# The involution's front joins the block of its taps, and the last experts' weight fold moves into it

## The chip, the cores and the metric

The kernel runs on one core of one Trainium2 chip. The metric is device time in microseconds (us) of one execution of the whole program. One execution was also recorded by the hardware profiler; its trace gives the span between the first and the last instruction, the busy time of each engine and what each instruction waited for. The engines are PE (matmuls), DVE (VectorE), ACT (ScalarE), POOL (GpSimd) and SP (which only issues DMAs here).

## The reference

Four layers, each a convolution-like mixer and then a mixture of experts, on 8 images of 64 channels and 32x32 pixels. The mixer of the last layer is an involution, and the experts of the last layer normalise their input and scale and shift it per expert:

```python
def _involution(x, w_reduce, w_span, gamma, beta):
    r = jnp.einsum('bchw,oc->bohw', x, w_reduce)
    mean = jnp.mean(r, axis=(0, 2, 3), keepdims=True)
    var = jnp.var(r, axis=(0, 2, 3), keepdims=True)
    r = (r - mean) * jax.lax.rsqrt(var + BN_EPS)
    r = r * gamma[None, :, None, None] + beta[None, :, None, None]
    r = jax.nn.relu(r)
    kern = jnp.einsum('bchw,kc->bkhw', r, w_span)          # 9 taps
    xp = jnp.pad(x, ((0, 0), (0, 0), (1, 1), (1, 1)))
    patches = jnp.stack([xp[:, :, i:i + H, j:j + W] for i in range(K) for j in range(K)], axis=2)
    return jnp.einsum('bckhw,bkhw->bchw', patches, kern)
...
# experts of the last layer
xe = xn[None, :, :] * ln_g[:, None, :] + ln_b[:, None, :]
h = jax.nn.gelu(jnp.einsum('end,edh->enh', xe, W1) + b1[:, None, :], approximate=False)
```

The mean and the variance run over all images and pixels, so nothing of the ReLU can begin before all of `r` is there.

## The kernel before, in words

The 8 images lie as 4 pairs (`Q` = 4; two images of 64 channels fill 128 partitions) of 1024 pixels, or as 8 tiles (`NT` = 8) of 512 columns. `X` is the running activation, `XN` its normalised copy; both stay in SBUF, as do all weights `W`.

The program is a row of blocks. In a block each engine has its own instruction list; at its end all engines meet at a barrier, and the next block begins. Inside a block the order on an engine is the written order, and engines wait for each other by counting semaphores.

Four blocks matter here.

**The scan of layer 2** (`mamba_scan`, L2056 to L2367). Its steps end with POOL's `gate`, and SP stores the result of the last image (L2099) and waits until it has landed (L2104). Behind its own scan work PE runs `fold_shift`: 16 matmuls with one moving column (L2041), which multiply the first-layer weights of the last experts by their shift `l3_b`. DVE then runs `fold_gain`: it adds that to the bias (L2049) and multiplies the weights by the gain `l3_g`, one instruction for each of the 8 experts (L2051). None of this is needed before the last experts.

**The involution's front** (a block of its own, L2543 to L2587). PE makes `r` for all 8 tiles in the 8 banks of PSUM (L2548). One ACT instruction copies all 4096 columns to `RR` and sums them (L2559); a matmul with `pairs` adds the sums over the partitions (L2553); DVE makes the negative mean (L2573); ACT squares (L2562); a second matmul; ACT takes the root (L2564), DVE inverts it with one Newton step and makes `SCALE` and `SHIFT` (L2575 to L2583, eight small instructions); one ACT instruction makes the ReLU of all 4096 columns, `RN` (L2566). POOL clears the padded image buffer `XP`.

**The block of the taps** is the block of the last experts (`deep_experts`), with the functions of `involution` called at the head of each engine's list. SP loads each pair's image into `XP` (L2597). For each pair `q` there are 18 taps `n`: two halves of 9, each on 512 columns. PE makes the tap's kernel in one of six PSUM banks (`kern`, L2614) and may run up to four taps ahead of DVE. DVE multiplies the shifted image by it (`scaled`, L2671); three taps (`OWN`) it adds itself (L2685), the others POOL adds (L2719). A half closes with DVE adding its own sum to `X` (L2692), then, after POOL's last addition, POOL's sum (L2694).

Between the taps of the last pair the engines prepare the first two tiles of the experts (`ahead(what, p)`): PE turns X (`in`, L1090), DVE centers (L1272, L1273), ACT squares (L1199), DVE inverts the deviation (`invert`, L1280 to L1298, 17 instructions), PE turns back (L1098), ACT copies (L1204), PE makes router logits (L1106), DVE ranks them (`rank`, L1308 to L1320, 14 instructions), ACT bends (L1209), DVE weighs (L1329 to L1333), PE and ACT turn the weights to rows (L1113, L1216).

**The experts**: PE `up` (L1135), ACT Gelu (L1236), PE `down` (L1158), DVE weighs the result (L1358), POOL adds it up (L1068). ACT's first Gelu waits for the last sum of the involution.

Of the kernel before, what the change touches and what calls it, by code (L numbers as in the profile page):

```python
# [99 lines left out]
def build(nc, x_dram, w_dram, seg_dram, out_dram):  # L100
    ctx = ExitStack()
    with ctx:
# [2433 lines left out]
        def involution():  # L2536
# [6 lines left out]
            with nc.Block() as block:  # L2543
                @block.tensor
                def _(pe):
                    mm = nc.tensor.matmul
                    for t in range(NT):
                        last = mm(PS[:, t, :], w("i_wr"), XN[:, t * T:(t + 1) * T], start=True, stop=True)  # L2548
                    last.then_inc(b_reduced.sem, 1)

                    for src, done in ((TOTAL, 1), (SS, 2)):
                        pe.wait_ge(b_total.sem, b_total.at(done))
                        mm(PS[:, 0, 0:1], w("pairs"), src, start=True, stop=True).then_inc(b_moment.sem, 1)  # L2553

                @block.scalar
                def _(act):
                    f = nc.scalar.activation
                    act.wait_ge(b_reduced.sem, b_reduced.at(1))
                    f(RR, PS[:, :, :].rearrange("p a b -> p (a b)"), ACT.Identity, accum_out=TOTAL)\  # L2559
                        .then_inc(b_total.sem, 1)  # L2560
                    act.wait_ge(b_chain.sem, b_chain.at(1))
                    f(RN, RR, ACT.Square, bias=NEGM, accum_out=SS).then_inc(b_total.sem, 1)  # L2562
                    act.wait_ge(b_moment.sem, b_moment.at(2))
                    f(SD, PS[:, 0, 0:1], ACT.Sqrt, bias=w("eps5")).then_inc(b_total.sem, 1)  # L2564
                    act.wait_ge(b_chain.sem, b_chain.at(9))
                    f(RN, RR, ACT.Relu, bias=SHIFT, scale=SCALE).then_inc(b_total.sem, 1)  # L2566

                @block.vector
                def _(dve):
                    v = nc.vector  # L2570
                    step = Chain(dve, b_chain).step
                    dve.wait_ge(b_moment.sem, b_moment.at(1))
                    step(v.tensor_scalar(NEGM, PS[:, 0, 0:1], -1.0, None, ALU.mult))  # L2573
                    dve.wait_ge(b_total.sem, b_total.at(3))
                    step(v.reciprocal(SD, SD))  # L2575

                    step(v.tensor_scalar(VAR, PS[:, 0, 0:1], w("eps5"), None, ALU.add))
                    step(v.tensor_tensor(SCALE, SD, SD, ALU.mult))
                    step(v.scalar_tensor_tensor(SCALE, SCALE, -0.5, VAR, ALU.mult, ALU.mult))
                    step(v.scalar_tensor_tensor(SD, SCALE, 1.5, SD, ALU.add, ALU.mult))  # L2580
                    step(v.tensor_tensor(SCALE, SD, w("i_gamma"), ALU.mult))
                    step(v.tensor_tensor(SHIFT, NEGM, SCALE, ALU.mult))
# [290 lines left out]
```

## Time and profile before

| | us |
|---|---|
| median of three runs | 1882.13 |
| lowest and highest of them | 1871.58, 1884.21 |
| the profiled execution, device time | 1880.6 |
| its span | 1878.8 |
| PE busy in the span | 1660.1 (88%) |
| DVE busy | 932.2 (50%) |
| ACT busy | 880.7 (47%) |
| POOL busy | 519.1 (28%) |

Busy time is an average over stages that differ. The stretches of the change, between 1118 and 1136 us, 1479 and 1510 us, and 1510 and 1617 us of the span, have to be read by themselves. The profiled execution lies 1.5 us under the median of the runs.

### The profile page before, as it was taken

How to read it: one execution, taken by the hardware profiler on the slowest of the kernel's cores; microseconds unless marked ns; L12 is line 12 of the kernel's file. 1: busy time of each engine (PE TensorE's matmuls, PEld its weight loads, DVE VectorE, ACT ScalarE, POOL GpSimd, SP SyncE). 2: the span in 40 equal slices, each digit the busy share in tenths (PEclk: the TensorE clock that was granted, in tenths of full speed). 3: DMA queues.
4: the chain of work that ended last, by engine and by line, in shares of the span. 5: the costliest groups of instructions: out<-in, count | busy, mean ns of one | idle time of the engine just before them, and what ended most of it. 6: DMA issues, size and time to landing. Idle time of an engine off the chain costs nothing. (4 is left out here: it accounts for less than half of the span.)

```text
span 1878.8 us, 50402 instructions
## 1 busy us (share of the span) xinstructions
PE 1660.1 (88%) x20792; PEld 759.1 (40%) x20792; DVE 932.2 (50%) x2080; ACT 880.7 (47%) x1185; POOL 519.1 (28%) x692
## 2 busy tenths in 40 slices
PE   7988999988998899789788887799999577799998
PEld 3553333333333332233677772333333233333332
DVE  3455544334665556430566654644442278645442
ACT  3225555554555355444445436355555500355554
POOL 0001222220000255501466651122323055122223
PEclk8899999998998799899899987899999799899999
DMA  5004232310000575258234312233232031242422
GB/s 246 12 12 90 48 78 59 71 21 34 12 1 23 124 159 124 50 198 294 63 111 140 125 42 90 46 65 73 54 84 46 0 34 11 50 93 52 94 60 63
DMA packets 88049, 143.24 MB, mean 76 GB/s; under 512 B 35256, under 2 KB 53816, under 8 KB 87824
## 3 DMA queue, kind: packets, MB, share of 16 engines
q1 hardware_dynamic: 87952, 142.02, 29.4%
q8 instruction: 52, 0.85, 0.2%
q14 instruction: 45, 0.37, 0.1%
HBM read 106.07 MB, written 25.44 MB: 70 GB/s over the span
## 5 line engine op out<-in xcount | busy, mean ns | idle before, releaser
L1236 ACT ACTIVATE ARENA<-PS,W 128x1024 f32<-128x1024 f32 x384 | 408.6, 1110 | 340.5 <-PE PS L1158 237.8
L1068 POOL TENSOR_TENSOR ARENA<-ARENA 128x512 f32<-128x512 f32 x168 | 213.0, 1268 | 729.8 <-DVE ARENA L1358 729.8
L1158 PE MATMUL PS<-ARENA,W 128*64 128x512 f32 x1536 | 350.8, 598 | 21.9 <-DVE ARENA L1358 21.9
L1135 PE MATMUL PS<-ARENA,W 64*128 64x512 f32 x1536 | 361.3, 609 | 1.9 <-DVE ARENA L1273 1.9
L1358 DVE SCALAR_TENSOR_TENSOR ARENA<-PS,W,ARENA 128x512 f32<-128x512 f32 x192 | 144.1, 750 | 328.4 <-PE PS L1158 314.0
L1158 PEld LDWEIGHTS PS<-ARENA,W 128*64 128x64 f32 x1536 | 101.9, 136 | 261.1 <-issue 218.6
L1135 PEld LDWEIGHTS PS<-ARENA,W 64*128 64x128 f32 x1536 | 141.1, 188 | 163.8 <-issue 109.0
L581 POOL TENSOR_TENSOR ARENA<-ARENA 128x512 f32<-128x512 f32 x56 | 71.0, 1268 | 292.7 <-DVE ARENA L913 291.1
L2338 PE MATMUL PS<-ARENA 32*32 32x32 f32 x8448 | 104.8, 196 | 6.7 <-issue 6.3
L751 ACT ACTIVATE ARENA<-PS,W 128x1024 f32<-128x1024 f32 x64 | 68.0, 1110 | 70.9 <-PE PS L655 70.9
L2338 PEld LDWEIGHTS PS<-ARENA 32*32 32x32 f32 x8448 | 93.7, 105 | 10.7 <-issue 7.3
L2614 PE MATMUL PS<-ARENA,W 128*128 (+1 forms) x144 | 75.1, 669 | 24.8 <-DVE ARENA L2671 17.3
L2208 ACT ACTIVATE ARENA<-PS 128x512 f32<-128x512 f32 x64 | 38.2, 597 | 94.3 <-PE PS L2312 94.3
L2719 POOL TENSOR_TENSOR ARENA<-ARENA 128x512 f32<-128x512 f32 x40 | 54.9, 1373 | 79.6 <-DVE ARENA L2671 78.1
L677 PE MATMUL PS<-ARENA,W 128*64 128x512 f32 x256 | 65.8, 625 | 8.4 <-DVE ARENA L913 8.4
L913 DVE SCALAR_TENSOR_TENSOR ARENA<-PS,W,ARENA 128x512 f32<-128x512 f32 x64 | 47.1, 749 | 50.8 <-PE PS L677 40.0
L1697 PE MATMUL PS<-ARENA 64*128 64x512 f32 x256 | 71.4, 656 | 0.6 <-ACT ARENA L1750 0.6
L655 PE MATMUL PS<-ARENA,W 64*128 64x512 f32 x256 | 70.3, 671 | 0.0
L1967 PE MATMUL PS<-XN,ARENA 64*128 64x512 f32 (+2 forms) x288 | 63.1, 592 | 4.1 <-DVE ARENA L2014 2.5
L368 PE MATMUL PS<-X,W 128*128 128x512 f32 x80 | 46.7, 694 | 20.0 <-PEq L306 7.2
L1750 ACT ACTIVATE ARENA<-PS 128x1024 f32<-128x1024 f32 x32 | 32.8, 1024 | 67.4 <-PE PS L1697 67.3
L1708 PE MATMUL PS<-ARENA 128*64 128x512 f32 x256 | 62.6, 605 | 0.4 <-ACT ARENA L1754 0.3
(244 smaller groups left out, 2256.3 us busy)
## 6 DMA issues: line engine op xcount, KB each, us to landing
ARENA<-scratch_g SPq DMA_DIRECT2D x64, 768.0 KB, 11.8
ARENA<-scratch_g SPq DMA_DIRECT2D x64, 256.0 KB, 5.9
W<-w_dram SPq DMA_DIRECT2D x1, 7307.5 KB, 24.6
ARENA<-XN SPq DMA_DIRECT2D x12, 512.0 KB, 3.7
ARENA<-XN SPq DMA_DIRECT2D x16, 256.0 KB, 11.2
scratch_x<-ARENA SPq DMA_DIRECT2D x8, 512.0 KB, 3.7
scratch_b<-ARENA SPq DMA_DIRECT2D x8, 512.0 KB, 4.0
scratch_z<-ARENA SPq DMA_DIRECT2D x8, 512.0 KB, 3.9
```

The source lines that it names most:

```text
L581: nc.gpsimd.tensor_tensor(SUM[:, k, :], SUM[:, k, :], TMP[:, e % 2, :], ALU.add)\
L655: last = mm(PS[:, (b % 2) * R + r, :], w(layer + "_w1", b * 128, (b + 1) * 128, half(r)), XE[half(r), k, :], start=True, stop=True)
L677: last = mm(PS[half(r), 4 + e % 2, :], w(layer + "_w2", b * C, (b + 1) * C), H[:, b % 4, r * T:(r + 1) * T], start=part == 0, stop=part == ...
L751: f(H[:, b % 4, :], PS[:, (b % 2) * R:(b % 2) * R + R, :].rearrange("p a b -> p (a b)"), ACT.Gelu, bias=w(layer + "_b1", b, b + 1)).then_i ...
L1068: nc.gpsimd.tensor_tensor(SUM[:, k, :], SUM[:, k, :], TMP[:, e % 2, :], ALU.add)\
L1135: last = mm(PS[:, (u % UPS) * R + r, :], w(layer + "_w1", b * 128, (b + 1) * 128, half(r)), XS[half(r), t % 2, :], start=True, stop=True)
L1158: last = mm(PS[half(r), out_of(e), :], w(layer + "_w2", b * C, (b + 1) * C), H[:, u % HS, r * T:(r + 1) * T], start=part == 0, stop=part = ...
L1236: f(H[:, u % HS, :], PS[:, at:at + R, :].rearrange("p a b -> p (a b)"), ACT.Gelu, bias=w(layer + "_b1", b, b + 1)).then_inc(e_gelu.sem, 1)
L1358: v.scalar_tensor_tensor(by_group(TMP[:, e % 2, :] if e else SUM[:, k, :]), by_group(PS[:, out_of(e), :]), w(layer + "_b2", e, e + 1), WB[ ...
L1697: last = mm(PS[:, 2 * r + h, :], XH[half(r), k, m * TOK:(m + 1) * TOK], XH[half(r), k, h * T:(h + 1) * T], start=True, stop=True)
L2338: last = mm(PS[g, MIXED + k, P + j * CHUNK:P + (j + 1) * CHUNK], XD[g, k, j, u * CHUNK:(u + 1) * CHUNK], M[g, k, u * P + j * CHUNK:u * P + ...
L2614: nc.tensor.matmul(PS[:, n % 6, :], w("i_ws", tap * P, (tap + 1) * P), RN[:, bass.ds(q * S + h * T, T)], start=True, stop=True)\
```

## The change

Three things are done. `fold_shift` and `fold_gain` leave the scan; they now run in the block of the taps, the matmuls in two parts. The front's block is gone: its work stands at the head of the engines' lists in the block of the taps. There the copy and sum are made tile by tile, the root by DVE from a bit pattern and three Newton steps, the ReLU pair by pair, and SP's loads of `XP` wait only for POOL's clearing. The preparation of the first tile is spread over the last two pairs.

```diff
-        def fold_shift(pe):
-            for b in range(E * HIDDEN["L3"]):
+        def fold_shift(part):
+            n = E * HIDDEN["L3"] // 2
+            for b in range(part * n, (part + 1) * n):
...
-            dve.wait_ge(f_shift.sem, f_shift.at(1))
+            dve.wait_ge(f_shift.sem, f_shift.at(2))
...
-                    fold_gain(dve)
...
-                    fold_shift(pe)
...
+                sp.wait_ge(b_cleared.sem, b_cleared.at(1))
+                sp.wait_ge(ln_scaled.sem, ln_scaled.at(0))
                 for k in range(2):
                     load(k, k)
...
+                for t in range(NT):
+                    mm(PS[:, t, :], w("i_wr"), XN[:, t * T:(t + 1) * T], start=True, stop=True)\
+                        .then_inc(b_reduced.sem, 1)
+                pe.wait_ge(b_total.sem, b_total.at(NT))
+                mm(PS[:, 6, 0:NT], w("pairs"), TOTAL, start=True, stop=True).then_inc(b_moment.sem, 1)
+                fold_shift(0)
+                pe.wait_ge(b_total.sem, b_total.at(NT + 1))
+                mm(PS[:, 7, 0:1], w("pairs"), SS, start=True, stop=True).then_inc(b_moment.sem, 1)
+                fold_shift(1)
+                pe.wait_ge(b_total.sem, b_total.at(NT + 2))
+                pe.wait_ge(f_done.sem, f_done.at(1))
+                with pe.Fori(0, Q - 2) as q:
+                    pe.wait_ge(b_total.sem, b_total.at(q + NT + 2))
+                    for n in range(BOTH):
+                        kern(q, n)
...
             def scalar(act, ahead):
+                f = nc.scalar.activation
+                for t in range(NT):
+                    act.wait_ge(b_reduced.sem, b_reduced.at(t + 1))
+                    f(RR[:, t * T:(t + 1) * T], PS[:, t, :], ACT.Identity, accum_out=TOTAL[:, t:t + 1])\
+                        .then_inc(b_total.sem, 1)
+                act.wait_ge(b_chain.sem, b_chain.at(1))
+                f(RN, RR, ACT.Square, bias=NEGM, accum_out=SS).then_inc(b_total.sem, 1)
+                act.wait_ge(b_chain.sem, b_chain.at(MOMENTS))
+                for q in range(Q):
+                    f(RN[:, q * S:(q + 1) * S], RR[:, q * S:(q + 1) * S], ACT.Relu, bias=SHIFT, scale=SCALE)\
+                        .then_inc(b_total.sem, 1)
...
+                dve.wait_ge(b_moment.sem, b_moment.at(1))
+                step(v.tensor_reduce(NEGM, PS[:, 6, 0:NT], AX.X, ALU.add, negate=True))
+                dve.wait_ge(b_moment.sem, b_moment.at(2))
+                step(v.tensor_scalar(VAR, PS[:, 7, 0:1], w("eps5"), None, ALU.add))
+                step(v.tensor_scalar(SD.bitcast(I32), VAR.bitcast(I32), 1, None, ALU.arith_shift_right))
+                step(v.tensor_scalar(SD.bitcast(I32), SD.bitcast(I32), -1, RSQRT_MAGIC, ALU.mult, ALU.add))
+                for n in range(3):
+                    step(v.tensor_tensor(NEWT, SD, SD, ALU.mult))
+                    step(v.scalar_tensor_tensor(NEWT, NEWT, -0.5, VAR, ALU.mult, ALU.mult))
+                    step(v.scalar_tensor_tensor(SD, NEWT, 1.5, SD, ALU.add, ALU.mult))
...
+                fold_gain(dve)
...
-                                ((1, "center", 0), (4, "invert", 0), (10, "rank", 0), (11, "center", 1),
-                                 (13, "weigh", 0), (15, "invert", 1)) if k else ())
+                                ((3, "weigh", 0), (5, "center", 1), (8, "invert", 1)) if k else
+                                ((2, "center", 0), (7, "invert", 0), (17, "rank", 0)))
...
+                pool.wait_ge(e_fold.sem, e_fold.at(0))
+                nc.gpsimd.memset(XP, 0.0).then_inc(b_cleared.sem, 1)
```

On DVE, at the end of the scan's block, the list before reads as follows (L2284 and L2288 are the scan's last steps, L2455 is the first of the next block):

```order
L2284 TENSOR_TENSOR ARENA<-PS,ARENA 128x128 [waits c_mixed]
L2288 SCALAR_TENSOR_TENSOR ARENA<-ARENA,W,PS 128x128 [waits c_summed]
L2049 TENSOR_TENSOR W<-W,PS 128x16 [waits f_shift]
L2051 TENSOR_SCALAR W<-W 128x256 x8
L2085 UNCONDITIONAL_BRANCH
L2451 UNCONDITIONAL_BRANCH [waits barrier_Pool_Activation_PE_DVE_SP_release]
L2455 TENSOR_SCALAR ARENA<-W 128x64
```

And the same place on DVE after the change (line numbers behind it are smaller by three):

```order
L2284 TENSOR_TENSOR ARENA<-PS,ARENA 128x128 [waits c_mixed]
L2288 SCALAR_TENSOR_TENSOR ARENA<-ARENA,W,PS 128x128 [waits c_summed]
L2085 UNCONDITIONAL_BRANCH
L2448 UNCONDITIONAL_BRANCH [waits barrier_Pool_Activation_PE_DVE_SP_release]
L2452 TENSOR_SCALAR ARENA<-W 128x64
```

The nine instructions of the fold stand between the front's chain and the first tap now.

On ACT, the front before, from the copy of `r` to the table of Gelu:

```order
L2559 ACTIVATE ARENA<-PS 128x4096 [waits b_reduced]
L2562 ACTIVATE ARENA<-ARENA 128x4096 [waits b_chain]
L2564 ACT_TABLE_LOAD
L2564 ACTIVATE ARENA<-PS,W 128x1 [waits b_moment]
L2566 ACTIVATE ARENA<-ARENA 128x4096 [waits b_chain]
L2543 UNCONDITIONAL_BRANCH
L1190 UNCONDITIONAL_BRANCH [waits barrier_Pool_Activation_PE_DVE_SP_release]
L2643 ACT_TABLE_LOAD
```

And after the change:

```order
L1190 UNCONDITIONAL_BRANCH [waits barrier_Pool_Activation_PE_DVE_SP_release]
L2625 ACTIVATE ARENA<-PS 128x512 [waits b_reduced] x8
L2628 ACTIVATE ARENA<-ARENA 128x4096 [waits b_chain]
L2631 ACTIVATE ARENA<-ARENA 128x1024 [waits b_chain]
L2631 ACTIVATE ARENA<-ARENA 128x1024 x3
L2633 ACT_TABLE_LOAD
```

The barrier and one table load between the two halves of the front are gone, and the long copy and the long ReLU are cut.

On PE, the last pair before (L2614 are taps, L1098 turns a tile back, L1106 makes logits, L1090 turns a tile in, L1113 turns the weights, L1135 is the first `up`):

```order
L2614 MATMUL PS<-ARENA,W 128x512 [waits i_scaled] x2
L1106 MATMUL PS<-W,ARENA 128x16 [waits ln_normed]
L1106 MATMUL PS<-W,ARENA 128x16 x3
L1090 MATMUL PS<-W,X 128x128 x4
L2614 MATMUL PS<-ARENA,W 128x512 [waits i_scaled] x6
L1113 MATMUL PS<-W,ARENA 64x128 [waits g_split]
L2614 MATMUL PS<-ARENA,W 128x512 [waits i_scaled] x2
L1098 MATMUL PS<-W,ARENA 128x128 [waits ln_scaled]
L1098 MATMUL PS<-W,ARENA 128x128 x3
L1106 MATMUL PS<-W,ARENA 128x16 [waits ln_normed,g_rows]
L1106 MATMUL PS<-W,ARENA 128x16 x3
L1135 MATMUL PS<-ARENA,W 128x512 [waits ln_normed,i_scaled]
```

And after the change, from near the end of the third pair (L2567 are taps; the first twelve below are the third pair's last two and the fourth pair's first ten):

```order
L1090 MATMUL PS<-W,X 128x128 x4
L2567 MATMUL PS<-ARENA,W 128x512 [waits i_scaled] x12
L1113 MATMUL PS<-W,ARENA 64x128 [waits g_split]
L2567 MATMUL PS<-ARENA,W 128x512 [waits i_scaled] x4
L1098 MATMUL PS<-W,ARENA 128x128 [waits ln_scaled]
L1098 MATMUL PS<-W,ARENA 128x128 x3
L2567 MATMUL PS<-ARENA,W 128x512 [waits i_scaled] x2
L1106 MATMUL PS<-W,ARENA 128x16 [waits ln_normed,g_rows]
L1106 MATMUL PS<-W,ARENA 128x16 x3
L2567 MATMUL PS<-ARENA,W 128x512 [waits i_scaled] x2
L1135 MATMUL PS<-ARENA,W 128x512 [waits ln_normed,i_scaled,f_done]
```

Before, all of the second tile's logits stood between the last tap and the first `up`; now two taps stand behind them. On DVE the fourteen instructions of `rank` stand behind the last tap of the third pair, and the seventeen of the second `invert` behind the ninth tap of the fourth, both ahead of the half's closing additions.

## Rows read from the trace of the kernel before

**Rows 1.** Timeline, end of the scan: start, us, engine, line, work, idle before.
```profile
1121.45 6.98 PE L2041 MATMUL PS<-W 64*128 64x1 f32 x32
...
1123.20 0.32 SPq L2099 DMA_DIRECT2D scratch_t<-ARENA  x1
...
1128.56 2.19 DVE L2051 TENSOR_SCALAR W<-W 128x256 f32<-128x256 f32 x8
...
1131.04 13.09 SPq L2389 DMA_DIRECT2D ARENA<-scratch_t  x8
```

**Rows 2.** Waits of SP's queue, 1100 to 1140: waiter, releaser, us, times, longest.
```profile
SPq L2085 <- PEq L2085: 4.9, 1, 4.9
```

**Rows 3.** Timeline, the front up to the first taps.
```profile
1479.04 10.00 PE L2548 MATMUL PS<-XN,W 128*128 128x512 f32 x16 [2.43 <-PEq L358]
...
1489.08 3.58 ACT L2559 ACTIVATE ARENA<-PS 128x4096 f32<-128x4096 f32 x1 [11.09 <-PE PS L2548]
...
1492.81 0.59 PE L2553 MATMUL PS<-ARENA,W 128*128 128x1 f32 x2 [3.76 <-ACT ARENA L2559]
...
1493.63 3.71 ACT L2562 ACTIVATE ARENA<-ARENA 128x4096 f32<-128x4096 f32 x1 [0.87 <-DVE ARENA L2573]
...
1499.10 0.17 DVE L2575 RECIPROCAL ARENA<-ARENA 128x1 f32<-128x1 f32 x1 [5.51 <-ACT ARENA L2564]
...
1500.72 3.80 ACT L2566 ACTIVATE ARENA<-ARENA 128x4096 f32<-128x4096 f32 x1 [1.72 <-DVE ARENA L2583]
...
1505.18 5.46 PE L2614 MATMUL PS<-ARENA,W 128*128 x8 [7.12 <-PEq L2543]
...
1510.28 3.08 DVE L2671 TENSOR_TENSOR ARENA<-ARENA,PS 128x512 f32<-128x512 f32 x5 [9.59 <-DMA ARENA<-XN]
```

**Rows 4.** Windows: stretch, length, busy of PE, PEld, DVE, ACT, POOL, PEclk, DMA, GB/s.
```profile
1121.40:1128.50 7.10, 7.03 (x41) 6.90 (x32) 0.58 (x3) 0.00 (x0) 0.91 (x2) 0.50 0.18 74
...
1479.00:1485.00 6.00, 5.96 (x7) 2.52 (x8) 0.00 (x0) 0.00 (x0) 2.02 (x1) 0.51 0.00 0
...
1489.00:1505.10 16.10, 1.22 (x5) 1.00 (x4) 1.50 (x9) 13.13 (x8) 0.00 (x0) 0.58 0.00 0
1505.10:1508.70 3.60, 3.52 (x4) 1.50 (x5) 0.00 (x0) 0.97 (x1) 0.00 (x0) 0.50 1.10 127
...
1521.70:1526.10 4.40, 4.34 (x6) 1.89 (x7) 4.33 (x7) 0.00 (x0) 2.54 (x2) 0.61 0.00 0
```

**Rows 5.** Timeline, starts of halves of the taps on DVE, and closing additions.
```profile
1532.75 3.07 DVE L2671 TENSOR_TENSOR ARENA<-ARENA,PS 128x512 f32<-128x512 f32 x5
...
1543.49 3.07 DVE L2671 TENSOR_TENSOR ARENA<-ARENA,PS 128x512 f32<-128x512 f32 x5
...
1551.36 1.04 DVE L2692 SCALAR_TENSOR_TENSOR X<-ARENA,X 128x512 f32<-128x512 f32 x1
...
1576.69 1.28 DVE L2671 TENSOR_TENSOR ARENA<-ARENA,PS 128x512 f32<-128x512 f32 x2
...
1593.13 1.28 DVE L2671 TENSOR_TENSOR ARENA<-ARENA,PS 128x512 f32<-128x512 f32 x2
...
1615.63 0.69 DVE L2694 SCALAR_TENSOR_TENSOR X<-ARENA,X 128x512 f32<-128x512 f32 x1 [1.23 <-POOL ARENA L2719]
```

**Rows 6.** Waits, 1500 to 1625.
```profile
DVE X L2694 <- POOL ARENA L2719: 9.8, 8, 1.2
```

**Rows 7.** Timeline: one instruction of `rank` twice, and POOL beside the first.
```profile
1594.49 1.26 POOL L2719 TENSOR_TENSOR ARENA<-ARENA 128x512 f32<-128x512 f32 x1 [2.07 <-DVE ARENA L2671]
1594.58 1.25 DVE L1309 TENSOR_TENSOR ARENA<-ARENA,W 128x64 f32<-128x64 f32 x1
...
1616.49 0.22 DVE L1309 TENSOR_TENSOR ARENA<-ARENA,W 128x64 f32<-128x64 f32 x1
```

**Rows 8.** Timeline, the first `up` matmuls and the first Gelu.
```profile
1615.08 8.78 PE L1135 MATMUL PS<-ARENA,W 64*128 64x512 f32 x32
...
1617.27 1.11 ACT L1236 ACTIVATE ARENA<-PS,W 128x1024 f32<-128x1024 f32 x1 [4.13 <-PE PS L1135]
```

More of the change, by code:

```diff
@@ L2540, in involution @@
             TMP, SUM, OSUM, OTMP = a.take(5, T), a.take(2, T), a.take(T), a.take(T)
-            TOTAL, NEGM, SS, SD, SCALE, SHIFT, VAR = (a.take(1) for _ in range(7))
+            TOTAL = a.take(NT)
+            NEGM, SS, SD, SCALE, SHIFT, VAR, NEWT = (a.take(1) for _ in range(7))
             ROWS_T = T // IMG
[L2543 to L2582, printed above, removed]
-                    step(v.tensor_tensor(SHIFT, SHIFT, w("i_beta"), ALU.add))
-                @block.gpsimd
-                def _(pool):
-                    nc.gpsimd.memset(XP, 0.0).then_inc(b_cleared.sem, 1)
@@ L2616, in kern @@
                         .then_inc(i_kern.sem, 1)
-                with pe.Fori(0, Q - 1) as q:
+                mm = nc.tensor.matmul
+                pe.wait_ge(ln_scaled.sem, ln_scaled.at(0))
+                for t in range(NT):
[3 more added lines that the diff above has]
+                mm(PS[:, 6, 0:NT], w("pairs"), TOTAL, start=True, stop=True).then_inc(b_moment.sem, 1)
@@ L2621, in tensor @@
+                last = Q - 2
                 ahead("in", 0)
-                for n in range(0, 8):
-                    kern(Q - 1, n)
+                for n in range(0, 13):
+                    kern(last, n)
                 ahead("back", 0)
-                kern(Q - 1, 8)
-                kern(Q - 1, 9)
+                kern(last, 13)
+                kern(last, 14)
                 ahead("logits", 0)
+                kern(last, 15)
                 ahead("in", 1)
-                for n in range(10, 16):
-                    kern(Q - 1, n)
+                kern(last, 16)
@@ L2631, in tensor @@
+                kern(last, 17)
+                last = Q - 1
+                for n in range(0, 10):
+                    kern(last, n)
                 ahead("turn", 0)
-                for n in range(16, BOTH):
-                    kern(Q - 1, n)
+                for n in range(10, 14):
+                    kern(last, n)
                 ahead("back", 1)
+                kern(last, 14)
+                kern(last, 15)
                 pe.wait_ge(g_rows.sem, g_rows.at(1))
                 ahead("logits", 1)
+                kern(last, 16)
@@ L2638, in tensor @@
+                kern(last, 17)
+                pe.wait_ge(f_done.sem, f_done.at(1 + E))
                 pe.wait_ge(i_scaled.sem, i_scaled.at(Q * BOTH))
@@ L2656, in vector @@
                 v = nc.vector
+                step = Chain(dve, b_chain).step
+                dve.wait_ge(b_moment.sem, b_moment.at(1))
[8 more added lines that the diff above has]
+                    step(v.scalar_tensor_tensor(SD, NEWT, 1.5, SD, ALU.add, ALU.mult))
+                step(v.tensor_tensor(SCALE, SD, w("i_gamma"), ALU.mult))
+                step(v.tensor_tensor(SHIFT, NEGM, SCALE, ALU.mult))
+                step(v.tensor_tensor(SHIFT, SHIFT, w("i_beta"), ALU.add))
+                fold_gain(dve)
                 def scaled(q, k, n, others):
```

2 lines of the change are left out of this document (added).

## The prediction

> **What bounds the kernel now.** PE is the busiest engine by far, but not in the stretches that change, so I read these by time: first the timeline of the scan's end, then SP's waits there, then the timeline and the clock windows of the involution's front, then the starts of the taps' halves on DVE with the waits that close them, and last the start of the experts. The reader is to see which engine comes last in each.
>
> At the scan's end it is the fold. PE's 16 fold matmuls take 6.98 us, from 1121.45 on, DVE multiplies weights until 1128.56 + 2.19 = 1130.75, and the next block's first DMA starts at 1131.04 [rows 1]. SP has been at the barrier for 4.9 us by then [rows 2], since 1126.1.
>
> In the front nothing runs beside anything: PE, then ACT, PE, DVE, ACT and so on from 1479.04 to 1510.28 [rows 3]. ACT's three passes over 4096 columns are 3.58, 3.71 and 3.80 us of it, and at the end DVE waits not for PE but for the loads of the padded image (idle 9.59, put down to the DMA).
>
> In the taps DVE leads. A half (9 taps) takes 1543.49 - 1532.75 = 10.74 us [rows 5], of which DVE waits 9.8 / 8 = 1.22 for POOL's last addition [rows 6]. The last pair's halves, which hold the preparation of the first two tiles, take 1593.13 - 1576.69 = 16.44 and, to the end of L2694 at 1616.3, 23.2 us [rows 5].
>
> **The change part by part.** The sum is made against the profiled execution, 1880.6 us.
>
> *The fold leaves the scan.* PE then ends at 1121.5, and SP comes last, at 1126.1. The release followed DVE's end by 1131.04 - 1130.75 = 0.29 us, so the next block starts at 1126.4: 4.6 us earlier. Bounds: 4.3 if the barrier takes twice as long behind SP, 4.9 if it takes nothing.
>
> *Front, copy by tiles.* PE needs 10.00 us for the 8 tiles as before. A float32 matmul is two passes in the rows. Seven took 5.96 us at the granted 0.51 [rows 4], 0.85 a pass and 1.7 a tile, the other nine the rest, 0.45 a pass and 0.9 a tile. ACT now follows tile by tile; an eighth of its 3.58 us is 0.45, with a fixed part some 0.6 to 0.8, less than a tile of PE, so only the last tile's stays behind PE: the first moment starts at 1489.8 instead of 1492.81. Gain 3.0.
>
> *Front, the root by DVE.* Before, from the square's start to the ReLU's it took 1500.72 - 1493.63 = 7.1 us. After: the square 3.71 and its read-out 0.2, a matmul of 0.59, and 15 small DVE instructions; eight of them took 1500.72 - 1499.10 = 1.62, 0.2 each, so 3.0. That is 7.5: a loss of 0.4. The ReLU starts at 1489.8 + 0.6 + 0.3 + 7.5 = 1498.2 instead of 1500.72.
>
> *Front, the ReLU by pairs, no barrier.* Only the first quarter is on the path: 3.80 / 4 = 0.95 and some 0.3 fixed, so the first tap's matmul can start at 1499.4 instead of 1505.18.
>
> *The fold in its new place.* Half of the matmuls are 6.98 / 2 = 3.5 us. The first half (1490.4 to 1493.9) lies beside the square, which ends at 1494.5; the second (1495.1 to 1498.6) beside DVE's 15 steps and the first ReLU, until 1499.4. The first tap waits for the bias addition too, and all of PE's taps are queued behind it; it comes at 1498.7, ahead of that ReLU. Then come DVE's 2.19 us of weight products, 1498.9 to 1501.1, while PE makes the first tap. Cost nothing; were that cover gone, 2.2.
>
> *The loads.* They took from the block's start, 1504.8, to 1510.28, 5.5 us. Now they are issued when POOL has cleared `XP`, early in the 20 us of the front; behind them SP has only the loads of the later pairs, which wait for DVE's products. POOL's clearing took 2.02 us, beside PE's first tiles [rows 4]; POOL has nothing else to do there. The 9.59 us are gone, and what is late next is PE.
>
> *PE's clock at the first taps.* Before, PE had four taps ready when the images came. It had made them at the granted 0.50 (1.2 GHz) for 3.6 us first [rows 4]: 1.7 us a tap instead of 0.9. Now DVE waits for each. If the low clock lasts 4.3 us (3.6 and 6.0 are the two rises in [rows 4]), taps 1 to 5 are there after 1.7, 3.4, 4.8, 5.7 and 6.6 us, and DVE ends the fifth at 1499.4 + 7.2 = 1506.6; before, five took 3.08 [rows 3], so that is as if DVE had started at 1503.5. Against 1510.28: **gain 6.8** for the whole front. Bounds: 6.0 with 6 us at the low clock, 9.1 with none (DVE is then held by the weight products).
>
> Here a rule bears. The row: while PE ran these very fold matmuls, busy for 7.03 of 7.10 us, the clock stayed at 0.50 [rows 4]. The Trainium skill says of the gate (TensorE: Matmul & The Clock Gate, "What's actually happening") that "activity releases the throttle"; by it the fold, now just ahead of the taps, would have raised the clock, and the front would gain 9.1. I take the row, and keep the rule as a rival.
>
> *The preparation over two pairs.* DVE's work is the same. In the last two halves it came to 16.44 - 10.74 = 5.7 and 23.2 - 10.74 = 12.5, 18.2 us; with eight plain halves, 85.9, and 2.0 for two halves that PE's clock lengthened (it had fallen, as at 1521.7, [rows 4]) that is the 106.0 from 1510.28 to 1616.3. Now the rank and the second invert stand between a half's last product and its closing additions, so POOL's last addition runs beside them: 1.22 of waiting goes twice, and L2692 runs without POOL beside it, 0.69 like L2694 instead of 1.04 [rows 5], twice. That is 3.1; PE's logits among the taps of the third pair may cost 0.3, and I leave the 2.0 for fallen clocks, since the rank and the inverts leave PE without taps for some us: **gain 2.8**. Bounds: 4.8 if no clock falls. Below nothing, since the moved pieces stand where POOL has additions queued: one instruction of rank took 1.25 beside POOL and 0.22 without [rows 7]; if three pieces lose that once more each, and 0.3 each to PE, it is 2.8 - 4.0 = -1.2.
>
> The row has a rule behind it: by the Trainium skill (SBUF — State Buffer, "Who interferes with whom") a DVE instruction with two SBUF inputs contends with a GpSimd one that reads SBUF. It agrees with the 1.25, and speaks against the new places; by it the taps would come to the lower bound.
>
> *The tail.* PE's first `up` started at 1615.08 behind the logits, and the first Gelu at 1617.27 [rows 8], 1.0 after DVE's last sum at 1616.3, for which ACT also waits. With two taps behind the logits, `up` starts with DVE's last product, some 2.5 us ahead of that sum, and Gelu starts on it: **gain 1.0**, at least 0.
>
> Sum: 4.6 + 6.8 + 2.8 + 1.0 = **15.2**; 1880.6 - 15.2 = 1865.4. The median is 1.5 above the profiled time, so 1866.9.
>
> **The rivals.**
>
> *The clock stays low in the taps (slower).* PE would then need 9 x 1.7 = 15.3 a half against DVE's 10.74 and be the bound: 72 taps take 122.4 us, and with some 6 for the preparation's matmuls and 1.3 for the last additions they end at 1499.4 + 129.7 = 1629.1, 12.8 after 1616.3. Less 4.6 for the scan that is 8.2 slower, 1890.3. It decides from 15.2 / (15.3 - 10.74) = 3.3 halves at the low clock on. For it: in the front PE's work is thin, 0.58 granted [rows 4], and the rank and inverts leave PE without taps for some us each. Against: the clock rose after 3.6 us of taps. 5%.
>
> *POOL blocks the moved preparation.* The taps then lose 1.2 instead of gaining 2.8: 1870.8. For it [rows 7], against it that both long pieces start when POOL has one or two additions left, which now hide behind them. 15%.
>
> *The clock is up at the first taps.* The 7 us of fold matmuls just ahead of them raise it; four taps are then made in 3.6 us, DVE is held by the weight products until 1501.1, and the front gains 9.1 instead of 6.8: 1864.6. Against it the 0.50 over the same matmuls [rows 4]. This is what the rule on the gate above would make of it. 12%.
>
> *The scan's end doesn't move,* because the store or something that the page doesn't show ends as late as the fold: no 4.6, 1871.5. Against it [rows 2]. 5%.
>
> **How the numbers follow.** The forecast has 60%; 3% are left for what I don't see. The bounds add to 4.3 + 6.0 - 1.2 + 0 = 9.1 and 4.9 + 9.1 + 4.8 + 1.0 = 19.8; 1882.1 less these is 1873.0 and 1862.3. The runs of before lie between 10.5 under and 2.1 over their median, so a median of a few runs may be some 4 off either way: 1858 to 1877, which holds all but the first rival and part of the rest. One per cent, 18.8 us, is about what a measurement of this kernel can tell from no change; the forecast is 0.8%. Faster by over 1% takes nearly all of the good ends at once or a median a few us lower: 28%. Slower by over 1% is the first rival at its worst, 4%.
>
> **What would show it.** In the trace after: the gate's first DMA 3.2 us behind the last store's issue instead of 7.8; the first tap's product some 22 us behind PE's first matmul of the front instead of 31.2; five products then spread over about 6 us; no wait for POOL behind the rank and the second invert; the first Gelu straight behind the last sum. I would be wrong if PE's granted clock is low for more than three halves, if the fold matmuls still run when the first ReLU is done, or if DVE's small instructions behind the ninth tap take 1 us each.

## The result and the profile after

The kernel after takes 1862.26 us (median of 8 runs, 1856.22 to 1870.59), the kernel before 1880.41 beside it (8 runs): ratio 0.9912, 95% interval 0.9883 to 0.9941, so 11 to 22 us less. The forecast was 1866.9 in 1858 to 1877. The profiled execution of after took 1869.24 us (span 1867.4, granted clock 0.941) against 1880.6: 11.4 less. Up to the scan's last store the two programs are the same, and there this execution is already 1.6 us late (1124.83 against 1123.20 in [rows 1]). So the change itself is read from stretches: 4.7 at the scan's end, 8.2 from PE's first matmul of the front to the first Gelu, 0.3 behind it, 13.2 in all, where the forecast had 15.2. One run of a later kernel (e3) took 2178.92 us at a granted clock of 0.725 and counts in no ratio below.

The timeline of after at the scan's end, against [rows 1, 2]:

```profile
1124.83 0.32 SPq L2099 DMA_DIRECT2D scratch_t<-ARENA  x1
...
1127.93 1.74 SPq L2386 DMA_DIRECT2D ARENA<-scratch_t  x4
1127.96 0.25 DVE L2452 TENSOR_SCALAR ARENA<-W 128x64 f32<-128x64 f32 x1 [4.22 <-PEq L2085]
```

From the last store's issue to the gate's first DMA it is 3.10 us instead of 7.84. DVE, which ended last before, now idles for 4.22 us; SP waits 2.3 us for its store to land and then 0.2 us for the release.

The front of after, against [rows 3]:

```profile
1476.13 10.05 PE L2574 MATMUL PS<-XN,W 128*128 128x512 f32 x16 [2.43 <-PEq L358]
...
1478.14 3.17 SPq L2548 DMA_DIRECT2D ARENA<-XN  x2
...
1486.96 0.39 PE L2577 MATMUL PS<-ARENA,W 128*128 128x8 f32 x2 [0.78 <-ACT ARENA L2625]
1487.28 2.13 PE L2041 MATMUL PS<-W 64*128 64x1 f32 x16
...
1487.59 3.71 ACT L2628 ACTIVATE ARENA<-ARENA 128x4096 f32<-128x4096 f32 x1 [0.68 <-DVE ARENA L2650]
1491.44 0.59 PE L2580 MATMUL PS<-ARENA,W 128*128 128x1 f32 x2 [2.03 <-ACT ARENA L2628]
1491.96 3.57 PE L2041 MATMUL PS<-W 64*128 64x1 f32 x16
...
1495.09 4.64 ACT L2631 ACTIVATE ARENA<-ARENA 128x1024 f32<-128x1024 f32 x4 [3.71 <-DVE ARENA L2661]
...
1495.72 2.19 DVE L2051 TENSOR_SCALAR W<-W 128x256 f32<-128x256 f32 x8
1496.78 14.27 PE L2567 MATMUL PS<-ARENA,W 128*128 x26 [1.25 <-DVE W L2051]
1498.96 0.69 DVE L2677 TENSOR_TENSOR ARENA<-ARENA,PS 128x512 f32<-128x512 f32 x1 [1.05 <-PE PS L2567]
...
1504.22 0.69 DVE L2677 TENSOR_TENSOR ARENA<-ARENA,PS 128x512 f32<-128x512 f32 x1 [0.17 <-PE PS L2567]
```

The first moment matmul stands 0.78 us behind PE's tiles, not 3.76. The loads of the image start 2.0 us into the front, and no row of DVE waits for a DMA. PE's wait ahead of the first tap is put down to DVE's weight products (L2051), which go on until 1497.9, behind the tap's start; of the fold it waits for the bias addition alone, done by 1495.8. What came last was the first quarter of the ReLU: the run without the fold below has the same first tap, at +20.64 against +20.65. First product at +22.8 instead of +31.2, and five products spread over 1498.96 to 1504.9.

Windows of the same stretch (columns as in [rows 4]):

```profile
1482.00:1486.30 4.30, 4.18 (x10) 1.52 (x8) 0.00 (x0) 3.15 (x11) 0.00 (x0) 0.99 1.59 140
1486.30:1489.50 3.20, 2.45 (x18) 2.34 (x18) 0.17 (x1) 2.52 (x3) 0.00 (x0) 0.90 0.00 0
1489.50:1496.70 7.20, 4.09 (x18) 3.98 (x18) 3.50 (x20) 3.49 (x4) 0.00 (x0) 0.50 0.00 0
1496.70:1502.60 5.90, 5.82 (x7) 2.52 (x8) 2.88 (x8) 4.32 (x4) 1.24 (x1) 0.50 0.00 0
1502.60:1511.00 8.40, 8.40 (x20) 3.42 (x18) 7.12 (x10) 0.00 (x0) 5.23 (x5) 1.00 0.00 0
```

The clock is high (2.4 GHz) in the later tiles and falls to 1.2 GHz while PE makes one-column matmuls and waits for ACT; the first taps run 5.9 us at the low level.

Closing sums of the last halves, and the tail, against [rows 5, 6, 8]:

```profile
1575.48 0.69 DVE L2700 SCALAR_TENSOR_TENSOR X<-ARENA,X 128x512 f32<-128x512 f32 x1
...
1593.31 0.69 DVE L2700 SCALAR_TENSOR_TENSOR X<-ARENA,X 128x512 f32<-128x512 f32 x1
...
1603.70 2.85 PE L1135 MATMUL PS<-ARENA,W 64*128 64x512 f32 x12 [1.46 <-issue]
...
1605.42 0.69 DVE L2700 SCALAR_TENSOR_TENSOR X<-ARENA,X 128x512 f32<-128x512 f32 x1 [1.23 <-POOL ARENA L2727]
...
1606.15 6.14 ACT L1236 ACTIVATE ARENA<-PS,W 128x1024 f32<-128x1024 f32 x6 [7.95 <-DVE X L2700]
```

The two sums behind the rank and the second invert wait for nothing, and the first Gelu starts on the last sum. But the added waits for PE and blocked small instructions are here too, and the experiments are to price them.

### The profile page after: what moved, and what is told of

Its sections match the earlier page's. It is cut to its first block and busy times, and to the rows that moved or that the text cites. A ratio compares the mean times of both kernels' runs of the same rounds, so it can differ in the third digit from the quotient of the medians.

```text
span 1867.4 us, 50393 instructions
## 1 busy us (share of the span) xinstructions
PE 1656.5 (89%) x20792; PEld 756.1 (40%) x20792; DVE 931.5 (50%) x2087; ACT 882.1 (47%) x1200; POOL 519.4 (28%) x692
## 5 line engine op out<-in xcount | busy, mean ns | idle before, releaser
L1135 PE MATMUL PS<-ARENA,W 64*128 64x512 f32 x1536 | 360.6, 607 | 4.1 <-DVE ARENA L1273 1.9
L1135 PEld LDWEIGHTS PS<-ARENA,W 64*128 64x128 f32 x1536 | 140.3, 187 | 166.7 <-issue 108.6
L2567 PE MATMUL PS<-ARENA,W 128*128 (+1 forms) x144 | 75.3, 667 | 27.7 <-DVE ARENA L2677 26.3
## 6 DMA issues: line engine op xcount, KB each, us to landing
ARENA<-XN SPq DMA_DIRECT2D x16, 256.0 KB, 10.8
```

Of the source, the lines that this page charges most:

```text
L1135: last = mm(PS[:, (u % UPS) * R + r, :], w(layer + "_w1", b * 128, (b + 1) * 128, half(r)), XS[half(r), t % 2, :], start=True, stop=True)
L2567: nc.tensor.matmul(PS[:, n % 6, :], w("i_ws", tap * P, (tap + 1) * P), RN[:, bass.ds(q * S + h * T, T)], start=True, stop=True)\
```

## The experiments

The runs of one kernel spread over some 6 to 16 us and go with the granted clock of the whole run (after's eight from 0.941 to 0.949). In the traces much of it lies ahead of every edit: the scan's last store is issued anywhere from 1113.25 (e11) to 1124.91 us (e7). So terms of 1 to 5 us are read from each kernel's own trace. The columns are us: last store's issue to the gate's first DMA; from PE's first matmul of the front to the first product, to the effective start, and to the first Gelu. Effective start is, as in the prediction, where DVE would have started the first half without waits: the start of DVE's own closing sum of that half (L2698 in after, 1509.37) less the 7.87 us that it takes from a half's first product to that sum in before. "Taps" runs from there to the end of the last sum.

| kernel | ratio to before (95%) | store to gate | first product | effective start | taps | first Gelu |
|---|---|---|---|---|---|---|
| before | 1 | 7.84 | 31.2 | 31.2 | 106.0 | 138.2 |
| after | 0.9912 (0.9883-0.9941) | 3.10 | 22.8 | 25.4 | 104.6 | 130.0 |
| e1 fold alone | 1.0001 (0.9977-1.0026) | 3.11 | 31.3 | 31.3 | 106.0 | 138.2 |
| e2 fold back | 0.9942 (0.9917-0.9967) | 7.85 | 22.8 | 25.4 | 104.6 | 130.0 |
| e3 preparation last | 0.9934 (0.9909-0.9959) | 3.10 | 22.8 | 25.4 | 105.0 | 131.3 |
| e4 whole passes | 0.9967 (0.9943-0.9990) | 3.09 | 27.2 | 28.7 | 105.5 | 134.2 |
| e5 extra matmuls | 0.9939 (0.9913-0.9966) | 3.11 | 22.7 | 23.4 | 105.3 | 128.7 |
| e6 rank later | 0.9928 (0.9902-0.9955) | 3.11 | 22.8 | 25.3 | 104.7 | 130.1 |
| e7 late sums | 0.9902 (0.9876-0.9928) | 3.09 | 22.8 | 25.4 | 98.2 | 123.6 |
| e8 late sums, extra matmuls | 0.9881 (0.9847-0.9915) | 3.09 | 25.1 | 26.4 | 99.7 | 126.1 |
| e9 late sums, mixed matmuls | 0.9881 (0.9849-0.9913) | 3.08 | 25.3 | 26.6 | 99.6 | 126.2 |
| e10 late sums, preparation last | 0.9900 (0.9868-0.9931) | 3.09 | 22.8 | 25.4 | 98.6 | 124.9 |
| e11 as e5 | one run | 3.09 | 22.7 | 23.3 | 105.2 | 128.6 |
| e12 as after | 0.9916 (0.9884-0.9948) | 3.08 | 21.6 | 24.2 | 104.6 | 128.8 |

**The fold alone (e1), and the fold back (e2).** In e1 the kernel before gets only the moved fold; in e2 the kernel after gets its fold back at the scan's end.

```diff
 # e1: before, in the front, behind each of the two moment matmuls
+                        fold_shift(done - 1)
...
 # e2: after
-                fold_shift(0)
...
-                fold_shift(1)
...
-                fold_gain(dve)
```

> The kernel before, with only the fold moved into the involution's front (its two parts behind the two moment matmuls, the weight products behind DVE's last small step). Theory: the scan's gain stands alone and the new place is free. From the last store's issue to the gate's first DMA 3.1 us instead of 7.8; from PE's first matmul of the front to the first product on DVE 31.2 us as before, since the loads end it; the clock at the first four taps may differ, but nobody waits for them. In all 4.7 us less. Rival, the fold delays the front: then the first product comes up to 7 us later and the sum is 0 or a loss.

> The kernel after, with the fold back at the scan's end and everything else as changed. Theory: from the last store's issue to the gate's first DMA 7.8 us again (4.7 more than after); the front is as in after within 0.3 us, the first tap's matmul 20.7 behind PE's first of the front and the first product 22.8, because the fold lay beside ACT and DVE. Rival, the fold matmuls just ahead of the taps do something for the clock: without them the clock is low for longer at the first taps, and DVE's effective start (end of its first half less 10.74) comes 1 to 3 us later than the 25.4 of after. Third: they cost something there (they end the first tap's wait); then the effective start comes up to 1 us earlier.

e1's stretches are as the theory has them: 3.11 at the scan's end, front and taps unchanged to 0.1 us. Its median shows no gain (the 4.7 us would be 0.9975, just outside its interval); nothing in its trace gives them back: the time from the first Gelu to the end is 261.57 against 261.53, and from the last store's issue to the end it is 751.0 us against 755.6 in before. So I put the median down to the scatter of whole runs, which is argued for the runs without a trace and not shown. e2 is the cleaner half. The timeline of its scan's end:

```profile
1117.67 6.98 PE L2041 MATMUL PS<-W 64*128 64x1 f32 x32
...
1119.41 0.32 SPq L2099 DMA_DIRECT2D scratch_t<-ARENA  x1
...
1127.26 1.74 SPq L2390 DMA_DIRECT2D ARENA<-scratch_t  x4
```

The wait of 7.85 is back, and from the front's first matmul to the first Gelu it takes 130.00 us against after's 130.02. PE's wait ahead of the first tap is put down to ACT's ReLU here, with the tap at +20.64 us as in after (+20.65). So the fold in its new place costs nothing. The window of its first taps (1497.48 on):

```profile
1497.40:1503.30 5.90, 5.82 (x7) 2.52 (x8) 1.67 (x3) 4.31 (x4) 1.23 (x1) 0.51 0.00 0
```

The same 5.9 us at the low level without the fold: it changes nothing about the clock there, so e2's rival and its third reading fall.

**One pass instead of tiles and pairs (e4).** The copy and the ReLU are single passes over 4096 columns; the steps that read their sums follow suit.

```diff
-                for t in range(NT):
-                    act.wait_ge(b_reduced.sem, b_reduced.at(t + 1))
-                    f(RR[:, t * T:(t + 1) * T], PS[:, t, :], ACT.Identity, accum_out=TOTAL[:, t:t + 1])\
-                        .then_inc(b_total.sem, 1)
+                act.wait_ge(b_reduced.sem, b_reduced.at(NT))
+                f(RR, PS[:, :, :].rearrange("p a b -> p (a b)"), ACT.Identity, accum_out=TOTAL[:, 0:1])\
+                    .then_inc(b_total.sem, 1)
...
-                for q in range(Q):
-                    f(RN[:, q * S:(q + 1) * S], RR[:, q * S:(q + 1) * S], ACT.Relu, bias=SHIFT, scale=SCALE)\
-                        .then_inc(b_total.sem, 1)
+                f(RN, RR, ACT.Relu, bias=SHIFT, scale=SCALE).then_inc(b_total.sem, 1)
```

> The kernel after, with ACT's copy and its ReLU each as one pass over 4096 columns instead of 8 tiles and 4 pairs. Theory: the first moment matmul starts 3.0 us later behind PE's front matmuls, and the first tap 2.7 us later behind DVE's last small step (3.8 for the whole ReLU instead of 1.0 to 1.3 for a quarter): PE's first matmul of the front to the first tap 26.4 us instead of 20.7. Of that all arrives at DVE, unless the clock at the first taps comes up differently: first product at about 28.5 instead of 22.8. Rival, something else than ACT holds the front (loads, the fold's bias or weight products): then the first product moves by less than 4 us.

In this execution PE's 16 matmuls of the front took 8.80 us instead of 10.05, since the clock was low there for 3.3 us (0.51) instead of some 6. e12, a second trace of after, is in the same case (8.80 us, 3.3 us at 0.50), and beside it the first tap comes 25.04 - 19.43 = 5.6 us later and the first product 27.2 - 21.6 = 5.6, as expected. The effective start moves by 4.5 only, since the first taps meet a shorter low clock. Windows of e4:

```profile
1499.00:1503.00 4.00, 4.00 (x6) 1.71 (x7) 0.94 (x2) 0.94 (x1) 0.00 (x0) 0.56 0.00 0
1503.00:1507.00 4.00, 4.00 (x11) 1.85 (x10) 3.45 (x5) 0.00 (x0) 2.55 (x2) 1.00 0.00 0
```

Of e12's gain of 31.2 - 24.2 = 7.0 us in the front, 4.5 are ACT's pieces; the rest is the loads, the barrier and the 1.25 of the faster tiles. No run parts the loads from the barrier, or tries the root on DVE alone.

**The clock at the first taps (e5, e11, e12).** `fill(5, n)` makes `n` matmuls of 512 columns into a PSUM bank that nobody reads then.

```diff
                 fold_shift(0)
+                fill(5, 2)
...
+                fill(5, 2)
                 fold_shift(1)
```

> The kernel after, with two more matmuls of 512 columns (results used by nobody) behind each of the two moment matmuls, so that PE is busy with wide matmuls beside ACT's square and DVE's small steps. They stand on PE ahead of the fold's parts and may push the first tap back by up to 1 us. Theory: the front lost 0.9 us against the forecast because the clock stayed at the low level for 5.9 us of taps; with a high clock at the first taps DVE's effective start comes 1.5 to 2.5 us earlier than after's 25.4 behind PE's first matmul of the front. Rival: two matmuls don't change the clock; then the effective start is the same or up to 1 us later.

> The kernel with two extra matmuls behind each moment matmul once more, for a second trace of the same code. Theory: whether the clock is up at the first taps depends on how its level happened to stand when the extra matmuls ran; the effective start is 23.4 or 26.4, not certainly 23.4. Rival: with DVE's halves at 10.7 the place is always good, 23.4 again.

> The kernel after itself once more, for a second trace and for times beside the others on the same chip. Theory: the front's clock at the first taps is as in the five other traces with the same front, effective start 25.4 and first Gelu 130.0 behind PE's first matmul of the front; the kernels with late sums are 5 to 7 us faster beside it.

The windows of e5 from the first extra matmuls on (first tap at 1497.31):

```profile
1488.40:1491.00 2.60, 2.60 (x8) 1.55 (x8) 0.00 (x0) 2.60 (x2) 0.00 (x0) 0.53 0.00 0
1491.00:1497.30 6.30, 5.26 (x25) 3.18 (x23) 3.37 (x20) 1.73 (x3) 0.00 (x0) 0.92 0.00 0
1497.30:1503.20 5.90, 5.89 (x14) 2.77 (x15) 5.26 (x12) 4.25 (x4) 2.54 (x2) 1.00 0.00 0
```

With the clock up, the effective start is 1.9 us behind the first tap (1499.2 against 1497.31); in after and e12 it is 4.7 to 4.8, in e4 3.6. So the low clock costs 2.8 us in after. The extra matmuls push the first tap itself back by 0.9 (+21.50 against +20.65), so 2.0 are left. It came out so twice (e5, e11), so e11's rival stands as far as two traces go. But 0.7 of the 2.0 are given back in the taps, where e5's third half takes 11.7 instead of 10.7 us, and the first Gelu is 1.3 earlier than after's. e12's effective start is not 25.4, as expected, but 24.2, all of it from PE's faster tiles; from the first tap on it is as in after. Beside it on the same chip the medians of e9 and e10 are 7.8 and 5.5 us lower.

**The place of the preparation (e3, e6).** e3 has it in the last pair in the order of before; e6 moves only the rank, behind the first product of the last pair.

```diff
 # e3, on DVE (and PE's pieces in the order of before)
-                                ((3, "weigh", 0), (5, "center", 1), (8, "invert", 1)) if k else
-                                ((2, "center", 0), (7, "invert", 0), (17, "rank", 0)))
+                                ((1, "center", 0), (4, "invert", 0), (10, "rank", 0), (11, "center", 1),
+                                 (13, "weigh", 0), (15, "invert", 1)) if k else ())
 # e6
+                                ((0, "rank", 0), (3, "weigh", 0), (5, "center", 1), (8, "invert", 1)) if k else
+                                ((2, "center", 0), (7, "invert", 0)))
```

> The kernel after, with the first tiles' preparation wholly in the last pair's second half and behind it, in the order of before, on PE and DVE. Theory: the stretch from the effective start to the end of the last sum goes from 104.6 back to 106.0 us (the forecast's gain of 2.8 was measured as 1.4), since two waits for POOL of 1.22 come back and two pieces no longer block beside POOL; the first Gelu stands 1.0 us behind the last sum instead of straight behind it. In all 2 to 3 us slower than after. Rival, the moved pieces gained nothing by themselves and the 1.4 is from something else: then this kernel is within 0.5 us of after in that stretch.

> The kernel after, with the rank of the first tile moved on DVE from behind the last product of the third pair to behind the first product of the fourth. Theory (POOL blocks a DVE instruction that starts beside it): POOL then still works on the last additions of the third pair and on the first of the fourth; the wait of 1.2 us ahead of that half's closing sum comes back, and one small instruction of the rank may still take over 1 us. The stretch from effective start to last sum 104.6 to 106.0. Rival, the place behind the last product was the bad one, since an instruction of 1.34 us stood there beside POOL: then the stretch is 0.3 to 1 us shorter.

DVE's waits in the last four halves (waiter, releaser, total, times, longest), first after, then e3:

```profile
DVE X L2700 <- POOL ARENA L2727: 3.7, 3, 1.2
DVE ARENA L2677 <- PE PS L2567: 3.3, 6, 1.1
```

```profile
DVE X L2691 <- POOL ARENA L2718: 6.1, 5, 1.2
DVE ARENA L2668 <- PE PS L2567: 0.3, 1, 0.3
```

The move takes 2.4 us of waits for POOL away, as the forecast said, and brings 3.0 of waits for PE. DVE's own instructions in the same stretch, again after and e3:

```profile
L2691 DVE TENSOR_TENSOR ARENA<-ARENA 128x512 f32<-128x512 f32 x8 | 7.6, 950 | 0.3
...
L2698 DVE SCALAR_TENSOR_TENSOR X<-ARENA,X 128x512 f32<-128x512 f32 x4 | 2.8, 688 | 0.2
```

```profile
L2682 DVE TENSOR_TENSOR ARENA<-ARENA 128x512 f32<-128x512 f32 x8 | 9.4, 1173 | 0.3
...
L2689 DVE SCALAR_TENSOR_TENSOR X<-ARENA,X 128x512 f32<-128x512 f32 x4 | 3.4, 861 | 0.0
```

Another 1.8 + 0.6 us less there, since fewer of these run beside POOL; but 0.4 more in the products, and some 0.9 more in small instructions that POOL blocks (L1331 and L1282 in after, L1287 in e3, L1309 in both). Sum: -2.4 + 3.0 - 1.8 - 0.6 + 0.4 + 0.9 = -0.5; the taps show -0.4 (105.0 to 104.6). In all e3 is 1.3 us behind after, not 2 to 3, and the rest of that is the tail: its first Gelu stands 0.95 behind the last sum, after's 0.04. Where the waits for PE come from, in the timeline of after:

```profile
1570.22 1.27 POOL L2727 TENSOR_TENSOR ARENA<-ARENA 128x512 f32<-128x512 f32 x1 [1.43 <-DVE ARENA L2677]
1570.23 1.34 DVE L1309 TENSOR_TENSOR ARENA<-ARENA,W 128x64 f32<-128x64 f32 x1
...
1576.82 5.36 PE L2567 MATMUL PS<-ARENA,W 128*128 128x512 f32 x7 [4.78 <-DVE ARENA L2677]
...
1578.98 1.17 DVE L1331 TENSOR_TENSOR ARENA<-ARENA 128x64 f32<-128x64 f32 x1
```

and in its windows:

```profile
1574.00:1576.80 2.80, 0.00 (x0) 0.00 (x0) 2.55 (x7) 0.21 (x1) 0.00 (x0) 0.54 0.00 0
1576.80:1580.00 3.20, 3.18 (x4) 1.52 (x5) 3.13 (x6) 0.00 (x0) 2.48 (x2) 0.50 0.00 0
```

While DVE ranks, PE has no free bank for 4.78 us, its clock falls, and the taps behind run at 1.2 GHz.

In e6 the blocked instruction (L1309) is short again, and the wait for POOL is back in its place (timeline, DVE):

```profile
1571.80 0.69 DVE L2700 SCALAR_TENSOR_TENSOR X<-ARENA,X 128x512 f32<-128x512 f32 x1 [1.23 <-POOL ARENA L2727]
...
1573.26 0.23 DVE L1309 TENSOR_TENSOR ARENA<-ARENA,W 128x64 f32<-128x64 f32 x1
```

L1309 is 1.1 us shorter, the wait 1.2 longer: the stretch is the same, 104.7, at the lower end of what the theory gave, and the rival's shorter one is not there. In after, behind the third pair, the block had eaten what the hidden wait gained.

**Late sums (e7), and with each of the others (e8 to e10).** POOL's sum of a half is added to the image behind the second product of the next half.

```diff
                         scaled(q, k, n, others)
+                        if tap == 1 and late:
+                            close(*late.pop())
...
-                    dve.wait_ge(i_added.sem, i_added.at(q * (2 * NADD) + (h + 1) * NADD))
-                    v.scalar_tensor_tensor(xt, SUM[:, h, :], 2.0, xt, ALU.mult, ALU.add)\
-                        .then_inc(i_done.sem, 1)
+                    late.append((q, h))
...
```

> The kernel after, with POOL's sum of each half added to the image one tap into the next half (behind its second product) instead of at the half's own end; the loop over pairs is unrolled for it. Theory: DVE's wait for POOL, 1.22 us at the end of each half, goes in the seven halves that have a successor; the plain halves take 9.5 us instead of 10.74, and the stretch from effective start to last sum 97 to 99 instead of 104.6; PE then has 9.5 us a half for taps that take 9 x 0.9 = 8.1 at the high clock. In all 5 to 8 us less. Rival, POOL itself is the bound (its additions fill a half): the wait only moves behind the second product, and the halves stay at 10.7. Second rival: PE becomes the bound where the clock falls; then 2 to 5 us.

> The kernel after, with both the late addition of POOL's sums and the two extra matmuls behind each moment matmul. Theory: the gains add, 5 to 8 us from the halves and 1.5 to 2.5 from the clock at the first taps. Rival: as for each of them alone.

A plain half in the timeline of e7 (DVE):

```profile
1519.11 1.04 DVE L2708 SCALAR_TENSOR_TENSOR X<-ARENA,X 128x512 f32<-128x512 f32 x1
1520.18 1.28 DVE L2677 TENSOR_TENSOR ARENA<-ARENA,PS 128x512 f32<-128x512 f32 x2
1521.39 0.68 DVE L2687 SCALAR_TENSOR_TENSOR X<-ARENA,X 128x512 f32<-128x512 f32 x1
...
1528.59 1.04 DVE L2708 SCALAR_TENSOR_TENSOR X<-ARENA,X 128x512 f32<-128x512 f32 x1
```

9.48 us instead of 10.74, with no wait: taps 98.2, first Gelu 6.4 us earlier, as expected. In e8 the extra matmuls did harm instead (windows; first tap at 1491.37):

```profile
1481.00:1484.00 3.00, 3.00 (x8) 1.83 (x8) 0.00 (x0) 2.64 (x2) 0.00 (x0) 0.51 0.00 0
1484.00:1488.00 4.00, 4.00 (x7) 1.77 (x6) 1.84 (x12) 0.00 (x0) 0.00 (x0) 0.52 0.00 0
```

The clock had fallen before them, as in e5, but it stayed low for 7 us though PE never paused. The second two took 3.1 us instead of e5's 2.0 and delayed the fold's second part and with it the first tap (+22.90), and the effective start is 26.4: the two gains of the theory don't add. e9 has one such matmul in the middle of each part of the fold and one behind the second:

```diff
                 if b % n == n // 2:
+                    fill(5, 1)
...
                 fold_shift(1)
+                fill(5, 1)
```

> The kernel with the late addition of POOL's sums, and with one unused matmul of 512 columns in the middle of each of the fold's two parts and one more behind the second part, so that no stretch of the fold's one-column matmuls is longer than some 1 us at the high clock. Theory: where the two extra matmuls behind the moments once brought the clock up (effective start 23.4) and once met a low clock (26.4), shorter thin stretches keep the clock of the front's wide matmuls; effective start 23 to 24 behind PE's first matmul of the front, first Gelu at 121.5 to 122.5 instead of 123.6. Rival: the clock falls at the fold all the same, and the extra matmuls then only push the first tap back: effective start 25.4 to 27, first Gelu 123.6 to 126.

26.6, first Gelu 126.2: the theory falls, the rival holds (by 0.2 beyond its end for the Gelu). The medians of e8 and e9 are the lowest of all (1855.57 and 1857.04), yet from PE's first matmul of the front to the first Gelu they are 2.5 us longer than e7; e8's gate starts 7.5 us earlier than e7's (1120.54 against 1128.00), ahead of every edit. By its stretches e7 is the best version, its first Gelu 6.4 us ahead of after's and 5.2 ahead of e12's; by whole times the three cannot be told apart.

e10 has late sums and e3's order of the preparation.

> The kernel with the late addition of POOL's sums, and with the first tiles' preparation in the last pair's second half again, on PE and DVE in the order of before. Theory: what the preparation gained from its new place are DVE's two waits for POOL (2.4 us), and what it lost there are 3.0 us of waits for PE; with late sums there is no wait for POOL to hide, so the old place is no worse in the taps: the stretch from effective start to last sum is 0 to 3 us shorter than the 98.2 of the late sums alone, and the first Gelu some 1 us behind the last sum. Rival: the waits for PE come from the preparation itself, wherever it stands; then the stretch is 98 to 100, and the first Gelu is 1 to 2 us later than 123.6.

98.6, first Gelu 124.9: my theory falls, the rival holds. Of DVE's waits in its last four halves, the longest:

```profile
DVE ARENA L2668 <- PE PS L2567: 3.4, 1, 3.4
```

The old order too makes DVE wait for PE once the waits for POOL are gone. In e3 it was the 6.1 us of waits for POOL that gave PE the time to catch up. So the preparation starves PE in either order, and whether DVE feels it depends on what else DVE waits for. Behind the first Gelu e10 loses another 1.6 us to e7: its first six Gelus take 7.7 us instead of 6.1, with waits for PE's `up` between them.

## Why the prediction held, and where its steps were off

**The fold leaves the scan: right.** 4.74 against 4.6, shown alone in e1 and in reverse in e2. SP did come last: its store's landing, then 0.2 us to the release, where [rows 1, 2] had given 0.29.

**The fold in its new place: right, with another split.** The two parts took 2.13 and 3.57 us rather than 3.5 each, the first at a granted clock of 0.90. e2 shows the price of zero. The rival that the fold raises the clock is out: 0.50 in after, 0.51 in e2. The Trainium skill's rule (TensorE: Matmul & The Clock Gate, "What's actually happening") was to make 9.1 of the front's gain. The trace disagrees for the fold: its second part kept PE busy for 3.57 us on end and was followed by 0.50, as its absence was by 0.51. The extra matmuls of e5 and e11 were followed by 1.00, as the rule has it, those of e8 by 0.54 at the first taps.

**Front: 5.9 instead of 6.8, mis-sized in the clock.** The steps up to the first tap came nearly as worked out, in us behind PE's first matmul of the front: first moment at +10.8 (10.8 forecast), ReLU at +19.0 (19.2), first tap at +20.65 (20.4). The term that failed is "if the low clock lasts 4.3 us": it lasted 5.9, so DVE's effective start lies 4.7 behind the first tap instead of 4.1. The lower bound of 6.0 had that case and was missed by 0.1, with the first tap's 0.3. No run reached the upper bound: with the clock up in e5 the front gains 7.9, not 9.1: the extra matmuls push the first tap back by 0.9, and it was 0.3 late already.

**Taps: 1.4 instead of 2.8, and for another reason.** The step that failed is "I leave the 2.0 for fallen clocks", the price of PE without taps. Of the 1.4, 1.0 comes from a plain half: before, the first two halves took 1532.75 - 1510.28 = 22.47 [rows 3, 5], the second 1.0 too long with the clock at 0.61 [rows 4]; after, and in e3, both are plain. This goes with the front (the second half takes 10.7 us in after, e2, e3, e6 and e12, and 11.7 in before and e1), but no term of the forecast had it: that much was luck. The moved preparation itself gives 0.4 (e3). Its two hidden waits for POOL are there (2.4) and so are the shorter sums (0.6, and 1.8 in DVE's additions that I had not counted), but PE's starved taps took 3.0 and POOL's blocking some 0.9, since the old order has two blocked instructions as well. My lower bound had the two the other way round, 3.1 for blocks and 0.9 for PE, so the rival on POOL was wrong in its mechanism, though the taps' gain fell toward its side.

The Trainium skill's rule for this (SBUF — State Buffer, "Who interferes with whom") agrees with L1309, 1.34 us beside POOL in after and 0.23 without in e6. By it the taps were to come to the lower bound of -1.2, and they did not.

**Tail: right.** 0.9 of the 1.0 (e3); the Gelu starts 0.04 behind the last sum.

**Rivals.** The clock did not stay low in the taps (1.00 from 1502.6 on in the first half); the scan's end moved. The 1870.8 of the rival on POOL is 1870.9 by its own terms. The forecast's 15.2 was 13.2 by the traces; that the median still fell lower than forecast (18.2 us under before's, 13.4 in e12's runs) I put down to the scatter of whole runs, which is larger than that error; this is argued, not shown.

## What to carry to other kernels

A hidden wait is only gained if nothing else was living on it: price a wait that is to go by what the other engines do in that time, here PE filling its banks while DVE waited for POOL. Work with no reader nearby can go beside a serial chain for nothing, and the proof is to put it back and see the chain unmoved. When whole runs scatter by 10 us, judge a change of 1 to 5 us by stretches between two fixed instructions, in several traces.

## What was not expected of the hardware

Extra wide matmuls are a gamble for the clock: the same ones, in the same front, gave 1.00 at the first taps in e5 and e11 and 0.54 in e8. PE was busy for 7.00 of 7.00 us in e8's two windows above and stayed at half speed. What sets the difference stays open; no run here varied it alone.

POOL also blocks DVE instructions with one tensor input: a 128x16 integer one (L1287) took 1.12 us in e10, ending with POOL's addition, and 0.17 in after.
